# A fused cross-attention and gene-mixing block on one core: a new order of work on all engines, PSUM by banks, and both LayerNorms centred on ScalarE

## The reference

```python
def _layernorm(x):  # eps 1e-05
    return (x - mean(x)) / sqrt(var(x) + eps)

# cross attention: 32 heads of 16, softmax over the tile's 128 context rows
q = rope(layernorm(x) @ Wq, pos); k, v = split(ctx @ Wkv); k = rope(k, pos)
w = softmax(q @ k.T * 0.25)                  # per head
x = x + (w @ v) @ Wout + bout

# gene mixing, on y = layernorm(x)
xn = y * rsqrt(mean(y * y) + eps) * norm_w
logits = xn @ Wc.T / clip(temperature, 0.1)  # 1024 genes
top_vals, top_idx = top_k(logits, 32)
expressed = softmax(top_vals) @ genes[top_idx]            # 64 wide
x = x + tanh(expressed @ Wd.T) * xn * (expressed @ Wu.T) * scale
```

## Time and profile before

| | us |
|---|---|
| median of 3 runs | 527.66 (527.11 to 529.24) |
| the profiled execution | 528.95 |
| its span, first to last instruction | 527.0 |
| TensorE busy | 457.6 (87%) |
| VectorE busy | 416.1 (79%) |
| GpSimd busy | 262.2 (50%) |
| ScalarE busy | 258.1 (49%) |

### The profile page before, as it was taken

The page is one execution under the profiler, slowest core; times in us unless marked ns, Lnnn a source line. Parts: engine busy times, 40 slices in busy tenths (PEclk is TensorE's granted clock), DMA queues, the critical chain, the costliest instruction groups (busy, mean ns, idle before and its releaser), DMA issues. The chain is left out here.

```text
span 527.0 us, 10932 instructions
## 1 busy us (share of the span) xinstructions
PE 457.6 (87%) x3866; PEld 336.8 (64%) x3866; DVE 416.1 (79%) x644; ACT 258.1 (49%) x386; POOL 262.2 (50%) x263
## 2 busy tenths in 40 slices
PE   1727698999999999999999999999999999796734
PEld 0525465677776767676777777777677776565523
DVE  3574274989898989899998989898989897866680
ACT  2641626374737374645555463647464737243111
POOL 0453527282919292928374655647382919110111
PEclk9967699999999999999999999999999999979776
DMA  7940504141322314050505050505041321200000
GB/s 266 283 90 18 95 1 89 25 87 26 69 64 51 84 30 103 21 109 21 109 21 109 21 109 21 109 9 113 9 92 38 73 59 37 65 23 1 21 20 21
DMA packets 81754, 34.45 MB, mean 65 GB/s; under 512 B 73136, under 2 KB 75200, under 8 KB 81728
## 3 DMA queue, kind: packets, MB, share of 16 engines
q1 hardware_dynamic: 80768, 33.05, 27.1%
q10 hardware_dynamic: 960, 1.05, 0.6%
HBM read 12.86 MB, written 4.19 MB: 32 GB/s over the span
## 5 line engine op out<-in xcount | busy, mean ns | idle before, releaser
L830 DVE MAX8 top<-stage_b 128x8 f32<-128x1024 f32 x64 | 78.0, 1218 | 32.3 <-ACT stage_b L579 32.1
L396 POOL TENSOR_TENSOR rstd<-var,minus_half 128x1 f32<-128x1 f32 x16 | 8.8, 550 | 178.1 <-DVE var L804 178.1
L838 DVE MATCH_REPLACE8 stage_b<-top,stage_b 128x1024 f32<-128x1024 f32 x64 | 77.3, 1208 | 0.0
L367 POOL TENSOR_TENSOR stage_b<-stage_b,cos_t 128x512 f32<-128x512 f32 x32 | 41.2, 1288 | 37.0 <-issue 25.5
L994 PE MATMUL gene<-wcT_h,yT_h 128*128 128x512 f32 x128 | 53.9, 421 | 1.1 <-DVE yT_l L817 1.1
L994 PE MATMUL gene<-wcT_l,yT_h 128*128 128x512 f32 x128 | 51.8, 405 | 0.0
L994 PE MATMUL gene<-wcT_h,yT_l 128*128 128x512 f32 x128 | 51.6, 403 | 0.0
L1101 PE MATMUL dense<-stage_a,v_ext 128*32 128x128 f32 x1024 | 42.6, 287 | 2.8 <-ACT stage_a L552 2.1
L536 ACT ACTIVATE parts<-turned 128x1024 f16<-128x1024 f32 x32 | 33.8, 1057 | 19.1 <-POOL turned L380 19.1
L765 DVE TENSOR_REDUCE row_max<-score_a 128x8 f32<-128x1024 f32 x32 | 38.9, 1217 | 4.8 <-PE score_a L1060 4.8
L765 DVE TENSOR_REDUCE row_max<-score_b 128x8 f32<-128x1024 f32 x32 | 38.9, 1215 | 3.7 <-PE score_b L1060 3.5
(11 more groups left out here) (149 smaller groups left out, 1129.2 us busy)
## 6 DMA issues: line engine op xcount, KB each, us to landing
x_ring<-x_dram SPq DMA_DIRECT2D x16, 256.0 KB, 2.6
out_dram<-x_ring SPq DMA_DIRECT2D x16, 256.0 KB, 2.5
ctx_sb<-ctx_dram SPq DMA_DIRECT2D x16, 128.0 KB, 2.5
stage_a<-L_ffn_Wc_dram SPq DMA_DIRECT2D x1, 2048.0 KB, 10.1
stage_b<-L_xattn_Wq_dram ACTq DMA_DIRECT2D x1, 1024.0 KB, 5.9
stage_b<-L_xattn_Wkv_dram SPq DMA_DIRECT2D x1, 1024.0 KB, 9.3
stage_b<-L_xattn_Wout_dram SPq DMA_DIRECT2D x1, 1024.0 KB, 12.5
genes_sb<-L_ffn_genes_dram SPq DMA_DIRECT2D x2, 256.0 KB, 5.2
```

The source lines that it names most:

```text
L367: pool.tensor_tensor(halves(qk_cos), halves(qk_sb), trig(cos_t, t), ALU.mult).then_inc(s_cosm[n], 1)
L830: nc.vector.max(top[:, 8 * n:8 * n + 8], logit if n == 0 else rest).then_inc(s_top[n], 1)
L838: nc.vector.match_replace(rest, top[:, 8 * n:8 * n + 8], logit if n == 0 else rest, REMOVED).then_inc(s_rem[n], 1)
```

## The change

1. The order of the calls in `iteration` is written anew on every engine, and the lags change. Scores of a tile are now taken in the iteration after its load (`t1`) rather than the one after that (`t2`), together with its `scoresT` and the first two groups of `values`; the other two groups follow early in the next iteration. On TensorE similar kinds stand together.
2. The four PSUM tensors are renamed to eight banks; each use has a bank or a pair of them (table `BANK`, `PAIR`), and the waits follow from it. `logits(t, 0)` and `logits(t, 1)` now share bank 5.
3. Both centrings go from VectorE to ScalarE (`center_x`, `center_y`), as mean minus x. The factor 1/std is no longer part of them: it is applied by ScalarE as the scale of `read_q` and `read_logits`, and for the second norm by GpSimd in `keep`, which was a copy and is a multiplication now. The signs are turned back in the weights.
4. Wk and Wv are loaded by two transfers, and split and released part by part; `center_x` no longer waits for `ln1`.
5. `express` takes its second half first. On SyncE and VectorE, register values for waits are computed at the head of the loop's body.

The new order on TensorE, and the core of the rest:

```diff
+        BANK = {"posT": 0, "down": 2, "eT": 2, "gene_wT1": 2, "row_maxT": 2, "yT": 2, "ctxT": 3,
+                "gene_wT0": 3, "xT": 3, "v": 4, "logits0": 5, "logits1": 5, "oT1": 5, "up": 5,
+                "oT0": 6, "q": 6, "attnT": 7, "k": 7, "proj": 7}
+        PAIR = {"duT": 0, "o": 0, "scores2": 0, "scores3": 0, "scoresT0": 0, "scoresT3": 0, "wcT1": 0,
+                "scores0": 1, "scoresT1": 2, "scoresT2": 2, "wcT2": 2, "scores1": 3, "wcT0": 3, "wcT3": 3}
...
+            def center_y(t):
+
+                hold(act)
+                act.wait_ge(s_mv2, t + 1)
...
+                nc.scalar.activation(yn[:], slot(t), ACT.Identity, bias=mv2[:, 0:1], scale=-1.0).then_inc(s_yn, 1)
...
-                pool.tensor_copy(kept_of(t), yn[:]).then_inc(s_kept, 1)
+                pool.tensor_tensor(kept_of(t), yn[:], rstd2[:].broadcast_to([P, DIM]), ALU.mult).then_inc(s_kept, 1)
...
-                nc.scalar.activation(logit[:, n * 512:(n + 1) * 512], gene[:, n * 512:(n + 1) * 512],
-                                     ACT.Copy).then_inc(s_lgr[n], 1)
+                act.wait_ge(s_norm2, t + 1)
+                nc.scalar.activation(logit[:, n * 512:(n + 1) * 512], logit_bank[n], ACT.Copy,
+                                     scale=rstd2[:]).then_inc(s_lgr[n], 1)
...
-            def norm2_apply(t):
...
-                nc.vector.tensor_scalar(yn[:], slot(t), mv2[:, 0:1], rstd2[:], ALU.subtract,
-                                        ALU.mult).then_inc(s_yn, 1)
```

More of the change, by code:

```diff
@@ L214, in rows_of @@
             return t[r:r + 64, (head // 2) * P:(head // 2 + 1) * P]
-        wcT_bank = (score_a, score_b, gene, score_a)
-        score_of = [score_a, score_b, score_a, score_b]
-        scoreT_of = [score_b, score_a, score_b, score_a]
+        wcT_bank = [pair(f"wcT{k}") for k in range(XK)]
+        score_of = [pair(f"scores{g}") for g in range(GROUPS)]
+        scoreT_of = [pair(f"scoresT{g}") for g in range(GROUPS)]
+        oT_bank = [bank(f"oT{n}") for n in range(2)]
+        logit_bank = [bank(f"logits{n}") for n in range(2)]
+        wT_bank = [bank(f"gene_wT{n}") for n in range(2)]
+        gene_out = [bank("down"), bank("up")]
         block = stack.enter_context(nc.Block())
@@ L229, in first, with only, upto, run @@
             return isinstance(t, int) and t == 0
+        def only(t, *tiles):
+            return isinstance(t, int) and t in tiles
+        def upto(t, tile):
+            return not (isinstance(t, int) and t > tile)
         def hold(eng):
             eng.wait_ge(s_trig, 1)
-        def run(eng, lags, iteration):
+        def run(eng, lags, iteration, counts=()):
             def tiles(i):
@@ L293, in next_x @@
             def next_x(t):
+                if not isinstance(t, int):
+                    for count in (t * 16, (t + 1 - XSLOTS) * 16):
+                        sp.to_reg(count)
                 sp.wait_ge(s_x, t * 16)
@@ L664, in _ @@
             duT_hi()
-            run(act, 5, iteration)
+            run(act, 6, iteration)
         @block.vector
@@ L940, in iteration @@
-                if t2 is not None:
-                    attn_lo(t2)
-                if t3 is not None:
-                    find_top(t3, 2)
+            angles()
+            constants()
+            norm1_stats(0)
+            for k in range(CK):
+                wk_lo(k)
+            for k in range(CK):
+                wv_lo(k)
+            ctx_lo(0)
+            for k in range(XK):
+                wq_lo(k)
             x_lo(0)
@@ L949, in _ @@
             scale_up()
-            norm1_apply(1)
-            wcT_lo(1)
-            for k in range(2, 4):
+            for k in range(1, 4):
                 wcT_lo(k)
@@ L1043, in scores @@
+                three_pass(bank("v"), (cT_h, cT_l), (columns(wkv_h, 512), columns(wkv_l, 512)), CK).then_inc(s_v, 1)
             def scores(t, g):
                 if g == 0:
-                    for n in range(2):
-                        pe.wait_ge(s_turned[n], 16 * (t + 1))
+                    if later(t, 1):
+                        pe.wait_ge(s_yT_l, t - 1)
+                    if only(t, 1):
+                        pe.wait_ge(s_nml, t)
+                elif g == 1:
+                    if later(t, 1):
+                        pe.wait_ge(s_x1, t - 1)
+                    if later(t, 14):
+                        pe.wait_ge(s_oT[0], t)
+                    if only(t, 1):
+                        pe.wait_ge(s_k_sb, t + 1)
+                    if upto(t, 14):
+                        pe.wait_ge(s_q_sb, t + 2)
+                elif g == 2:
+                    pe.wait_ge(s_turned[0], (t + 1) * 16)
+                    pe.wait_ge(s_turned[1], (t + 1) * 16)
+                    if first(t):
+                        pe.wait_ge(s_split_duT, 1)
@@ L1153, in transpose_w @@
+                for g in range(4):
+                    last = nc.tensor.transpose(wT_bank[n][:, g * P:(g + 1) * P],
+                                               gene_w[:, n * 512 + g * P:n * 512 + (g + 1) * P], ident[:])
                 last.then_inc(s_wT[n], 1)
             def express(t):
-                pe.wait_ge(s_wTr[0], t + 1)
                 pe.wait_ge(s_wTr[1], t + 1)
```

712 lines of the change are left out of this document (378 added, 334 removed).

## The result

| | before | after |
|---|---|---|
| median of 4 runs each | 528.2 (527.1 to 529.2) | 508.8 (507.2 to 511.3) |
| profiled execution / its span | 528.95 / 527.0 | 507.2 / 505.4 |
| TensorE, VectorE, ScalarE, GpSimd busy | 458, 416, 258, 262 | 433, 387, 274, 257 |

The ratio is 0.9637 (95% interval 0.9592 to 0.9682). The new kernel is faster, but by 19 us where 34 were forecast, and 0.8 us outside the forecast range of 484 to 508. After, `transpose_o` is L1204, a pass L1073, `scores` L1150, `values` L1194, the search L917.

A forecast was written before the change was run, and what follows sets the result against it. TensorE's queue was taken as the bound, VectorE 2.8 us a tile behind. Span 38.4 (first scores) + 57 (fill) + 12 x 25.7 (loop) + 89.1 (drain) = 492.9 us; forecast time 494, range 484 to 508.

The forecast's parts named there:

- 23.9 of content: TensorE's queue, one tile: passes, fp16 groups, transpositions, `values` and `express` take 23.9 us.
- 1.3 of borders: TensorE, per tile: 10 changes of the array part in use, down from 17, at 0.13 us each.
- 0.5 of waits: TensorE, per tile: all new waits together, such as second exponential and shared logits bank, taken as 0.5 us.
- my own signs of being wrong: Loop: step over 26.7, longest TensorE waits for maxima, `aT_l` or logits' read, clock under 1.00; ends not some 10 us shorter.
- 3 us of slack: VectorE in the loop: 22.6 us of work a tile, below the new step of 25.7 by 3 us.
- rival 1: VectorE takes over: it and GpSimd add 1 us a tile, step 26.7, time 506; chance 0.22.
- Rivals 2 and 4: 2: waits only move, drain gains but 3, 514 us, chance 0.07. 4: gaps lower the loop's clock, 536 us, chance 0.04.
- rival 3: Loop: even the 0.5 us of waits is absent, GpSimd gains; step 25.2 or less, 488 and under; chance 0.13.
- I take 0.9 us off (0 to 2): 38.4: Set-up: first scores start at 38.4 instead of 39.29, as Wk lands earlier and `center_x` waits for no power.
- 14, 20 and 23 us for iterations 1 to 3, 57 in all: Fill, first scores to start of the fifth iteration: 57 us laid out link by link, against 55.9 before.
- The sum is 89.1: Drain: iteration 16 at 23.3, iteration 17 at 21.6, then 16.9 and 27.3; 89.1 us against 99.8 before.
- I take 16.9, as the search of tile 14 starts earlier: Drain, end of iteration 17 to the first search of tile 15: 16.9 us against 18.1 before.

The follow-up runs named there:

- two_borders: The new kernel with `logits(t, 0)` cut in two halves and `scores(t, 0)` between them, 12 borders a tile instead of 10: 517.0 us.
- centre_on_dve: The new kernel with both centrings back on VectorE, the factor 1/std staying where the new kernel has it: 530.9 us.
- x_lo_early: The new kernel with VectorE splitting x of tile 1 right behind the last part of Wc, ahead of `wout_lo` and `duT_lo`: 506.5 us.
- setup_order: The new kernel with `x_lo(1)` early and the set-up in the order of its chain, context and x split ahead of the weights on ScalarE: 503.5 us.
- warm_fill: `setup_order` with 41 superfluous f32r passes in six waits of TensorE between `project_q(1)` and `project_v(1)`: 502.8 us.
- ctx_first: `setup_order` with the context transposed and `project_k` done right behind `project_q` for tiles 1 to 3, ahead of the previous tile's scores: 511.2 us.
- k_early: `all_together` with own banks for context transposition and `project_k` in tiles 1 and 2, and k's rope and split in the same iteration: 497.3 us.
- warm_drain: The new kernel with 7 to 9 superfluous f32r passes in four waits of TensorE in the last two iterations with `project_out`: 504.5 us.
- exp_table_early: The new kernel with one small exponential on ScalarE behind `x_hi(1)`, so that the table load stands in an earlier wait: 508.8 us.
- attn_lo_first: The new kernel with VectorE doing `attn_lo` ahead of the search `find_top(1)` instead of behind it: 507.0 us.
- all_together: The new kernel with `setup_order`, early exponential table, `attn_lo` first, superfluous passes in fill and drain, and `logits(15, 1)` in bank 6: 494.8 us.

## Why the prediction was right and wrong

The profiled span came out at 505.4 instead of 492.9: 4.1 by the first scores, 4.3 by the way from there to the fifth iteration, -0.5 by the twelve iterations, 4.5 by the drain. The median lies 1.6 above the profiled execution, which was the fastest of its four, where I had carried over 1.3 below: 2.9 of the 14.8 us between forecast and measurement are in this alone.

**Right, with its size: the step.** Forecast 23.9 of content, 1.3 of borders and 0.5 of waits, 25.7; measured 25.66. The first two sum to 25.2, and that is the step of the written-out iterations, 25.24, with `two_borders` giving 0.13 a border. The 0.5 was right by luck: I meant it for the second exponential and the shared bank, which cost nothing in the loop, and it is the loop's edge on VectorE reaching TensorE through `aT_l`, 0.56 us in nine of the twelve iterations. That wait was one of my own signs of being wrong, and it is TensorE's only one there.

**Right: the centrings.** VectorE fell to 23.0 (22.6 forecast), ScalarE rose to 16.1 (16.6), and without this part the step is 26.96. Two small prices were off: a centring on ScalarE takes 0.72 to 0.77 us instead of 0.69, and "Scales on reads that exist anyway cost nothing" does not hold, since `read_logits` takes 0.69 with its scale and took 0.60 without. What I did not see is how little room the forecast left: I gave VectorE 3 us of slack, it idles 2.7 in the new kernel, and `centre_on_dve`, where it sets the step, still idles 2.3 (`cT_h` at 1.3 above all). So rival 1 was nearer than its 22% said, and the loop's wait is its small form. Rivals 2 and 4 did not come: no new wait for maxima, clock 1.00. The 25.2 of rival 3 is the step of the written-out iterations only.

**Wrong: "I take 0.9 us off (0 to 2): 38.4".** The first scores came at 42.54. The step named Wk's earlier landing and Wout's split. It did not count `project_q(1)`, which the new order puts ahead of `scores(0, 2)`, nor follow what that waits for in VectorE's queue. `x_lo_early` shows 3.05 us of it; `setup_order`, which also puts the chain of the first scores ahead of the other splits, takes out 6.15.

**Wrong: "14, 20 and 23 us for iterations 1 to 3, 57 in all".** Measured 16.0, 20.8 and 24.5, 61.3 in all. The link-by-link sum follows one chain and has no term for the clock. The clock was 0.70 in 40 to 60 us, and passes in the waits shorten the first round by 3.1 us in `warm_fill`, where it was 0.53 without them. Moving k's chain ahead lengthens a round, the second of `ctx_first` by 2.4 us and the first of `k_early` by 3.2. How much of the 4.3 us belongs to each, in the new kernel itself, stays open.

**Wrong: "The sum is 89.1".** Iteration 17 was right (21.3 against 21.6). Iteration 16 took 24.6 (23.3), the stretch to the search of tile 15 19.6 (16.9), the rest 28.1 (27.3). The step that failed for the stretch is "I take 16.9, as the search of tile 14 starts earlier": it takes 1.2 off the old stretch and has no term for the clock behind the new waits. Two groups of twelve passes ran at the lower level there, 1.6 us more each. `warm_drain` makes the stretch 16.55 us, so these 3.1 are the clock and the rest of the term was right; the shared bank's 0.78 are in it with and without the passes. I had the number in hand, 0.88 in iteration 17 of the kernel before, and used it for a rival only. In iteration 16 the clock was 0.93; in `exp_table_early`, with the same instructions and 1.00, the iteration takes 23.1, so its 1.3 are the clock as well. What made the rest 0.8 us longer stays open.

## What to carry to other kernels

Ask of a reordering and of an offloading together which engine binds after each one: here each alone left the time where it was, and both took 19 us. Price the fill and drain with the clock they will have and follow every instruction that the new order puts ahead of the first useful one, into the queue of the engine that it waits for. A few per cent of the run can be had back there with cheap means.

## What the runs showed of the hardware

- The granted clock of a stretch with gaps is not fixed by the instructions in it. The same ones, about iteration 17, ran at 1.00 in the new kernel, at 0.86 in `setup_order` and at 0.84 in `exp_table_early` and `attn_lo_first`; between the last two `transpose_o` it is 21.7 us in the first and 24.2 to 24.4 in the others, so some 2.5 us of a gain made earlier are given back. In iteration 16 it is the other way round: 0.93 in the new kernel and 1.00 in `exp_table_early`, 24.6 us against 23.1. What decides it was not found. These are single profiled executions, and the clock differs between executions of one kernel too: the mean over the span is 0.944 to 0.954 in the four of the new kernel, lowest in the slowest.
- Seven to nine superfluous passes in waits of about 2 us of the drain keep the granted clock at 1.00 (2.4 GHz) where it was 0.83, and TensorE idles at most 0.26 us between them and the work behind them.
- One turn of the hardware loop leaves VectorE idle for 0.5 us where it closes behind a short instruction (0.15 us), and not at all where it closes behind a search (1.2 us). The written-out iterations show nothing there.
- f32r next to f32 costs nothing also in the loop (0.24 us from the last pass of `logits` to `transpose_o`, at 297.67 and 297.91); a border of array shapes costs 0.13.
- The issue of one transposing transfer of kT holds SyncE's queue, mostly for 2.5 us (1.5 to 3.5 in the new kernel, 4.3 for the first one of `all_together`), and the next context's load stands behind it: 208.55 to 211.06, and the load at 211.26.
